# Eight expert groups on one core: slots turned between the up halves, 256-column up products, rank sums shared with VectorE

## What is computed

```
mod = silu(c) @ wmod -> sa, ca, ga, sb, cb, gb       (ga, gb pushed away from 0)
h = layernorm(x) * (1 + ca) + sa ;  x = x + ga * attention(h)     (causal, one head of 256)
h = layernorm(x) * (1 + cb) + sb ;  x = x + gb * ffn(h)

ffn(h):  scores = sigmoid(h @ gate_w.T); best 2 of 4 groups, best 4 of their 16 experts
         weight of a rank = 2 * score / sum of the four scores
         expert e (32 of them, at most 64 tokens each):
             out = (silu(t @ w1[e]) * (t @ w3[e])) @ w2[e]     w1, w3: 256x128, w2: 128x256
         + shared expert: silu(h @ shared_gate) * (h @ shared_up) @ shared_down   (256 wide)
```

## Time and profile before

| what | us |
|---|---|
| median of 3 runs | 176.83 |
| the three runs | 175.35, 176.83, 176.85 |
| the profiled execution | 175.42 |
| its span (first to last instruction) | 173.7 |
| busy in the span: PE, DVE, ACT, POOL | 147.5, 108.9, 62.4, 55.4 |
| first `expert_up` starts | 116.42 |
| first map matmul of the tail (L1391) starts | 153.33 |
| last DVE operation starts | 171.09 |

### The profile page before, as it was taken

One profiled execution on the slowest core, in us unless ns is written; L12 is line 12 of the kernel. 1 busy time (PEld: TensorE's weight loads), 2 busy tenths in 40 slices (PEclk: granted clock), 3 DMA queues, 4 the chain that ended last, 5 costly groups with the idle time before them and its releaser, 6 DMA issues.

```text
span 173.7 us, 2811 instructions
## 1 busy us (share of the span) xinstructions
PE 147.5 (85%) x938; PEld 102.1 (59%) x938; DVE 108.9 (63%) x386; ACT 62.4 (36%) x167; POOL 55.4 (32%) x77
## 2 busy tenths in 40 slices
PE   0198769999999899997598969996999989879993
PEld 0153534887547767685274624886666656568882
DVE  2679964836955688799884598382566664321563
ACT  3257578633055526375243623012333333200000
POOL 7319700499500000000000000777077776440000
PEclk9999999999999999999999999999999999999999
DMA  4999999999999942001000110244113331118995
GB/s 130 340 321 405 423 400 357 348 349 347 349 348 348 348 136 70 0 0 38 30 4 0 44 60 4 68 123 115 36 37 101 94 73 69 50 46 298 411 319 181
DMA packets 21808, 31.34 MB, mean 180 GB/s; under 512 B 2032, under 2 KB 17942, under 8 KB 21794
## 3 DMA queue, kind: packets, MB, share of 16 engines
q1 hardware_dynamic: 20354, 27.71, 46.8%
q0 software_dynamic: 1440, 3.45, 7.2%
HBM read 23.65 MB, written 8.26 MB: 184 GB/s over the span
## 4 chain that ended last, share of the span: by engine, by line
PE 50%; DVE 32%; ACT 7%; issue 5%; DMA 3%; SPq 1%; DVEq 0%; ACTq 0%
PE bank L1054 16%; PE bank L1351 10%; PE bank L1397 6%; PE bank L1391 4%; DMA w_sb<-in_L_wmod_dram 3%; PE bank L1370 3%; DVE bmax L797 3%; DVE st L708 2%; DVE rows L818 2%; PE bank L1184 2%; PE bank L1361 2%; DVE base L811 2%; PE bank L1328 2%; PE bank L1158 2%; PE bank L1162 2%
## 5 line engine op out<-in xcount | busy, mean ns | idle before, releaser
L444 POOL DMA_INDIRECT arena<-token_rows,gather_idx x16 | 16.4, 1025 | 67.2 <-DVE gather_idx L907 62.6
L1351 PE MATMUL bank<-w_sb,arena 128*64 128x128 f32 x256 | 17.3, 278 | 3.4 <-ACT arena L655 1.3
L1351 PEld LDWEIGHTS bank<-w_sb,arena 128*64 128x64 f32 x256 | 13.9, 136 | 7.7 <-issue 4.1
L453 POOL DMA_INDIRECT results<-aT,res_idx x14 | 14.0, 999 | 11.0 <-DVE aT L997 7.9
L1184 PE MATMUL bank<-arena 128*128 128x256 f32 x72 | 17.2, 382 | 0.3 <-issue 0.3
L1184 PEld LDWEIGHTS bank<-arena 128*128 128x128 f32 x72 | 13.1, 190 | 2.5 <-issue 0.9
L1054 PE MATMUL bank<-w_sb,h2T 128*128 128x512 f32 x12 | 7.6, 769 | 8.2 <-DMA w_sb<-in_L_wmod_dram 8.2
L1017 DVE TENSOR_TENSOR h2T<-h2T,bank 128x256 f32<-128x256 f32 x8 | 3.4, 421 | 15.7 <-ACT h2T L672 15.7
L537 ACT ACTIVATE prob<-bank,nmax 128x512 f32<-128x512 f32 (+3 forms) x12 | 6.9, 581 | 12.4 <-DVE nmax L801 12.4
L1397 PE MATMUL bank<-w_sb,ident 128*128 128x256 f32 x48 | 10.6, 382 | 0.0
L556 ACT ACTIVATE h2T<-bank,modc 128x128 f32<-128x128 f32 x16 | 6.4, 455 | 11.5 <-PE bank L1192 11.5
(11 more groups left out here) (154 smaller groups left out, 302.2 us busy)
## 6 DMA issues: line engine op xcount, KB each, us to landing
w_sb<-in_L_ffn_w_dram SPq DMA_DIRECT2D x12, 1024.0 KB, 12.3
results<-prob SPq DMA_DIRECT2D x1, 4096.0 KB, 16.7
w_sb<-results SPq DMA_DIRECT2D x7, 512.0 KB, 6.4
token_rows<-rows SPq DMA_DIRECT2D x8, 144.0 KB
xin<-in_L_attn_x_dram SPq DMA_DIRECT2D x4, 256.0 KB, 4.3
w_sb<-in_L_wmod_dram SPq DMA_DIRECT2D x1, 1024.0 KB, 9.5
out_dram<-base SPq DMA_DIRECT2D x8, 128.0 KB, 3.7
w_sb<-in_L_attn_qkv_dram SPq DMA_DIRECT2D x1, 768.0 KB, 7.1
```

The costliest lines, as they stand in the source:

```text
L444: nc.gpsimd.indirect_dma_start(out=slot_in[:, r, :], out_offset=None, in_=rows_d, in_offset=bass.IndirectOffsetOnAxis(ap=gather_idx[:, r:r ...
L453: nc.gpsimd.indirect_dma_start(out=results_d, out_offset=bass.IndirectOffsetOnAxis(ap=res_idx[:, r:r + 1], axis=0), in_=ob[:, g % 4, (r % ...
L1351: last = t.matmul(bank[4 + g % 2][CAP * side:CAP * side + CAP, o:o + F], slotT[:, k, CAP * e:CAP * e + CAP], w[:, e, k, :], start=(k == 0) ...
```

## The change

- `w1_sb` and `w3_sb` become one buffer `w13_sb` in which w1 and w3 of an expert stand side by side; an up product moves 256 columns (w1 and w3 at once, two pieces of 128 columns that lie 256 floats apart), 16 records for a group in place of 32.
- PE's order in a group is now: `expert_up(g, 0)`, `turn_hid(g - 1)`, `turn_slots(g + 1)`, `expert_up(g, 1)`, `expert_down(g - 1)`. ACT and DVE turn `slot_evac(g + 1)` ahead of silu and product. The copies of scores and `score_sums` stand behind DVE's product.
- `shared_down(3)` goes to the last group, in halves, one on each side of `turn_hid(7)`; for that `ob` gets buffers of its own, and the banks of `SHD_BANK` change.
- `positions(2)` and `map_slots(1, ...)` each stand one `shared_up_part` later.
- POOL gathers groups 0 to 5 ahead of the first give_back (`AHEAD` = 5).
- In the tail PE adds two ranks (three for the last tile), DVE two (one for the last); the maps go over tiles 1 to 7 and then 0.

```diff
--- before.py
+++ after.py
@@ -70,8 +70,7 @@
-        w1_sb = sb("w1_sb", [P, E, KT, F])
-        w3_sb = sb("w3_sb", [P, E, KT, F])
+        w13_sb = sb("w13_sb", [P, E, 2, KT, F])
         w2_sb = sb("w2_sb", [P, E, H])
...
-        flat = lambda t, k: t.rearrange("p e k f -> p (e k f)") if k else t.rearrange("p e n -> p (e n)")
-        place1, place3, place2 = flat(w1_sb[:, last_q], 1), flat(w3_sb[:, last_q], 1), flat(w2_sb[:, last_q], 0)
+        place13 = w13_sb[:, last_q].rearrange("p e w k f -> p (e w k f)")
+        place1, place3 = place13[:, 0:2048], place13[:, 2048:4096]
+        place2 = w2_sb[:, last_q].rearrange("p e n -> p (e n)")
         wmod_a = place3[:, 0:1024].rearrange("p (k n) -> p k n", k=KT)
@@ -136,7 +136,7 @@
         slotT = take(KT * E * CAP).rearrange("p (k s) -> p k s", k=KT)
-        ob = aT[:, :, :].rearrange("p f n -> p (f n)").rearrange("p (b s) -> p b s", b=4)
+        ob = [take(512) for _ in range(3)] + [aT[:, 0, 0:512]]
         silu_c = h2T[:, 0, 0:256].rearrange("p (k n) -> p k n", k=KT)
...
-        yin = [w1_sb[:, 4 * i:4 * i + 4].rearrange("p e k f -> p (e k f)") for i in range(NT)]
+        yin = [w13_sb[:, 2 * i:2 * i + 2].rearrange("p e w k f -> p (e w k f)") for i in range(NT)]
         sh_act = prob[:, :, :].rearrange("p b n -> p (b n)").rearrange("p (b n) -> p b n", n=512)
@@ -302,7 +302,8 @@
         SH_BANK = {key: bank[b] for key, b in zip(SH_ORDER, (0, 1, 2, 3, 6, 4, 5, 0))}
-        SHD_BANK = [bank[b] for b in (1, 2, 4, 5)]
+        SHD_BANK = [bank[b] for b in (1, 2, 3, 0)]
+        PE_RANKS = [2] * (NT - 1) + [3]
         esum = sb("esum", [P, NT, 2])
@@ -354,10 +355,9 @@
                     sp.wait_ge(qT_mm, 2)
-                sp.dma_start(w1_sb[:, e], w1[e].rearrange("e (p k) f -> p e (k f)", k=KT)
-                             .rearrange("p e (k f) -> p e k f", k=KT)).then_inc(experts_loaded[g], 16)
-                sp.dma_start(w3_sb[:, e], w3[e].rearrange("e (p k) f -> p e (k f)", k=KT)
-                             .rearrange("p e (k f) -> p e k f", k=KT)).then_inc(experts_loaded[g], 16)
+                for what, w_d in enumerate((w1, w3)):
+                    sp.dma_start(w13_sb[:, e, what], w_d[e].rearrange("e (p k) f -> p e (k f)", k=KT)
+                                 .rearrange("p e (k f) -> p e k f", k=KT)).then_inc(experts_loaded[g], 16)
                 sp.dma_start(w2_sb[:, e], w2[e].rearrange("e p n -> p e n")).then_inc(experts_loaded[g], 16)
@@ -452,10 +452,10 @@
                         out=results_d, out_offset=bass.IndirectOffsetOnAxis(ap=res_idx[:, r:r + 1], axis=0),
-                        in_=ob[:, g % 4, (r % 2) * H:(r % 2 + 1) * H], in_offset=None,
+                        in_=ob[g % 4][:, (r % 2) * H:(r % 2 + 1) * H], in_offset=None,
                         bounds_check=N * TOPK - 1, oob_is_err=False).then_inc(returned[g % 4], 16)
-            AHEAD = 4
+            AHEAD = 5
             for g in range(EGROUPS):
@@ -666,13 +666,13 @@
                     hid_evac(g - 1)
+                if g + 1 < EGROUPS:
+                    slot_evac(g + 1)
                 act.wait_ge(up_mm, g + 1)
...
                              ACT.Silu).then_inc(silu_done, 1)
-                if g + 1 < EGROUPS:
-                    slot_evac(g + 1)
             hid_evac(EGROUPS - 1)
@@ -975,64 +975,75 @@
             shared_add(1)
-            score_sums()
-            shared_add(2)
...
                 dve.wait_ge(slotT_mm, g + 1)
+                v.tensor_scalar(slotT[:, 1, 256 * g:256 * g + 256], bank[1][:, 0:256],
+                                modc[:, 0, 1:2], modc[:, 1, 1:2], ALU.mult, ALU.add).then_inc(slotT_dve, 1)
+
+            def scores_of_slots(g):
+
                 for side in range(2):
...
                                        slot_flat[half, (2 * g) * (ROW + 2) + H + side::ROW + 2][:, 0:2]))
-                v.tensor_scalar(slotT[:, 1, 256 * g:256 * g + 256], bank[1][:, 0:256],
-                                modc[:, 0, 1:2], modc[:, 1, 1:2], ALU.mult, ALU.add).then_inc(slotT_dve, 1)
-
...
-
-            slot_evac(0)
-            shared_add(3)
-            dve.wait_ge(base_done, NB)
-            dve.wait_ge(scale_done, 1)
-            for g in range(EGROUPS):
+
+            def expert_hid(g):
+
                 dve.wait_ge(silu_done, g + 1)
...
                                 ALU.mult).then_inc(hid_done, 1)
-                if g + 1 < EGROUPS:
-                    slot_evac(g + 1)
-                if g >= 1:
+
+            def expert_evac(g):
+
+                dve.wait_ge(down_mm, g + 1)
+                if g >= 4:
+                    dve.wait_ge(returned[g % 4], 16 * 2 * (g // 4))
+                settle()
+                for r in range(2):
+                    last = v.scalar_tensor_tensor(out=ob[g % 4][:, H * r:H * r + H], in0=bank[6 + g % 2][:, H * r:H * r + H],
+                                                  scalar=slot_score[:, 2 * g + r:2 * g + r + 1], in1=mod[:, 5, :],
+                                                  op0=ALU.mult, op1=ALU.mult)
+                last.then_inc(ob_done, 1)
+
...
+
+            slot_evac(0)
+            shared_add(2)
+            for g in range(EGROUPS - 1):
+                slot_evac(g + 1)
+                expert_hid(g)
+                scores_of_slots(g)
+                if g == 0:
+                    score_sums()
+                else:
                     expert_evac(g - 1)
...
                     back_map(2 * g - 1)
+            scores_of_slots(EGROUPS - 1)
+            expert_evac(EGROUPS - 2)
+            expert_hid(EGROUPS - 1)
             expert_evac(EGROUPS - 1)
-
+            shared_add(3)
+            dve.wait_ge(base_done, NB)
+            dve.wait_ge(scale_done, 1)
...
                     dve.wait_ge(y_rest_loaded, 16)
-                chain(v.scalar_tensor_tensor(out=base[:, i, :], in0=yin[i][:, H * 3:H * 4],
-                                             scalar=scale2[:, i:i + 1], in1=base[:, i, :], op0=ALU.mult, op1=ALU.add))
+                for k in range(PE_RANKS[i], TOPK):
+                    chain(v.scalar_tensor_tensor(out=base[:, i, :], in0=yin[i][:, H * k:H * k + H],
+                                                 scalar=scale2[:, i:i + 1], in1=base[:, i, :], op0=ALU.mult, op1=ALU.add))
                 dve.wait_ge(sum_mm, i + 1)
@@ -1284,16 +1295,17 @@
-            def shared_down(j):
+            def shared_down(j, parts=(0, 1)):
...
                     pe.wait_ge(sh_silu, 2)
-                for i in range(2):
+                for i in parts:
                     tok = slice(P * (2 * j + i), P * (2 * j + i) + P)
...
                                                                      for f in range(FS // P)])
-                last.then_inc(shd_mm, 1)
+                if 1 in parts:
+                    last.then_inc(shd_mm, 1)
@@ -1304,11 +1316,11 @@
             shared_up_part(SH_ORDER[5])
+            shared_up_part(SH_ORDER[6])
             positions(2)
-            shared_up_part(SH_ORDER[6])
-            map_slots(1, BATCHES[2][0], NT, 3)
             pe.wait_ge(sh_silu, 1)
             shared_up_part(SH_ORDER[7])
+            map_slots(1, BATCHES[2][0], NT, 3)
             pe.wait_ge(shd_scaled, 1)
@@ -1321,7 +1333,7 @@
                     pe.wait_ge(ridx_done, 1)
-                    pe.wait_ge(base_done, 2)
+                    pe.wait_ge(base_done, 1)
                     pe.wait_ge(sh_hid, 4)
@@ -1329,34 +1341,30 @@
-            def expert_up(g):
-
-
-                if g % 2 == 0:
-                    pe.wait_ge(experts_loaded[g // 2], 48)
-                pe.wait_ge(slotT_act, g + 1)
-                pe.wait_ge(slotT_dve, g + 1)
-                if g >= 2:
-                    pe.wait_ge(hid_done, g - 1)
-                else:
-                    pe.wait_ge(base_done, 3 + g)
-                for r in range(2):
-                    for what, w in enumerate((w1_sb, w3_sb)):
-                        if g >= 1 and (r, what) == (1, 1):
-                            turn_hid(g - 1)
-                        o = 256 * r + P * what
-                        for k in range(KT):
-                            for side in range(2):
-                                e = 4 * g + 2 * r + side
-                                last = t.matmul(bank[4 + g % 2][CAP * side:CAP * side + CAP, o:o + F],
-                                                slotT[:, k, CAP * e:CAP * e + CAP], w[:, e, k, :],
-                                                start=(k == 0), stop=(k == KT - 1))
-                last.then_inc(up_mm, 1)
+            def expert_up(g, r):
+
+                if r == 0:
+                    if g % 2 == 0:
+                        pe.wait_ge(experts_loaded[g // 2], 48)
+                    pe.wait_ge(slotT_act, g + 1)
+                    pe.wait_ge(slotT_dve, g + 1)
+                    if g >= 2:
+                        pe.wait_ge(hid_done, g - 1)
+                for k in range(KT):
+                    for side in range(2):
```

(41 more changed lines are left out.)

13 lines of the change are left out of this document (6 added, 7 removed).

## The result

The changed kernel takes 170.62 us (median of four, 170.51 to 172.6), the kernel before, run beside it, 176.6 (175.35 to 176.85): ratio 0.9701, 95% interval 0.9617 to 0.9786. The forecast was 170.5. The profiled execution took 170.63 us with a span of 168.9; the forecast for that span was 168.0.

The account below looks back on a forecast made before the run. PE was taken to bound the expert loop and the tail, there nearly tied with loads. Terms took 5.7 us off the span, giving 169.7 us profiled or 171.1 against the median; forecast 170.5, range 168.0 to 174.0.

Parts of the forecast that it names:

- The order ahead of the experts: Work before the expert loop: filling PE's two idle gaps brings the first up block forward, gain 1.1 us.
- One group: Expert loop: PE pays columns, not records; fewer width changes and no slot wait cut the period from 4.44 to 3.5 us.
- A rule that speaks for more: PE's matmuls: 60 cycles overhead per record would bring an estimated 3.2 us; given no part in the forecast.
- Gathers: POOL's calls run without idle; PE stalls 0.8 us at `turn_slots(7)`; maps at 147.7, where they were at 153.33.
- The tail: Final sums after the maps: DVE takes PE's place at 1.42 us a tile, so the moved rank gains nothing.
- The sum: Whole kernel: 5.7 us off the span, 173.7 to 168.0; profiled execution 175.4 to 169.7; forecast 170.5.
- two bases: Starting points for the whole time: the profiled execution gives 169.7 us, the median of runs 171.1.
- A period of 4.0 (1): Expert loop: hidden part or DVE's queue sets the group, 4.0 us; time 172.4 to 173.2; chance 0.17.
- the second base: Whole time reckoned from the median of the runs shown instead of the profiled execution: 171.1 us.
- Loads setting the tail (2): Tail: loads and PE, not DVE, set the pace; time 168.1 to 169.5 us; chance 0.13.
- The strided operand (3): Up products: two-piece moving operand runs below one column a step; slower, 183.5 us if pairs double; chance 0.06.
- POOL's calls (4): Gathers and give_backs stretch to 1.5 us each from 1.32, cancelling the early gain; within 1%; chance 0.05.

Follow-up runs that it names:

- front_old: Changed kernel with `positions(2)` and `map_slots(1, ...)` each one `shared_up_part` earlier, as before the change: 169.38 us, ratio to the kernel before 0.9591.
- before_up256: Kernel before with only `w13_sb` and 256-column up products, order, gathers and tail as before: 176.77 us, ratio to the kernel before 1.0007.
- down128: Changed kernel with `expert_down` products cut into two of 128 columns, 64 more matmul records: 170.88 us, ratio to the kernel before 0.9709.
- order_old: Changed kernel with `turn_slots(g + 1)` behind `expert_up(g, 1)` and `slot_evac` behind `expert_hid(g)` again: 181.48 us, ratio to the kernel before 0.9499.
- ranks3: Changed kernel with PE adding three ranks of every tile in the tail and DVE one, as before: 182.33 us, kernel before beside it 191.6.
- best: Changed kernel with `shared_down(3)` halves around `turn_slots(0)`, PE ranks two and three by turns, six gathers ahead: 178.41 us, ratio to the kernel before 0.9354.
- ahead6: Changed kernel with `AHEAD` = 6 in place of 5: 182.67 us, kernel before beside it 191.6.
- up128_b: Changed kernel with 128-column up products, run a second time, now beside the unmodified changed kernel: 187.74 us, ratio to the kernel before 0.9864.
- the third comparison: Runs on a chip without the long unnamed waits: the unmodified changed kernel 170.79 us, the kernel before 176.62 us, and three edited kernels.
- ahead4: Changed kernel with `AHEAD` = 4 in place of 5: 183.37 us, kernel before beside it 191.6.
- up128: Changed kernel with each 256-column up product cut into two of 128, 32 records a group: 189.37 us, ratio to the kernel before 0.9897.
- the first comparison: First set of follow-up runs, editing products, ranks and gathers ahead, beside the kernel before at 191.6 us, without the unmodified changed kernel.
- after_again: The changed kernel, unmodified, rerun beside the kernel before at 190.71 us: 179.9 us, ratio 0.9414.

## Why the prediction was right

**The order ahead of the experts.** Right in mechanism, small errors in size. The forecast had `positions(2)` late by 0.25 us; PE starts it 0.13 us behind the reduction's end (104.15 + 0.80 to 105.08), where it was 0.05: late by 0.08. `turn_slots(0)` waits for the first gather, as said, and the first up block starts 116.29 - 104.15 = 12.14 us behind the reduction, where it was 13.51: 1.37 us gained, 1.1 forecast. But the step counted this as a gain at the end as well, through group starts set by PE, while giving 0.8 us of it back at `turn_slots(7)`. front_old shows that all of it is given back. I had the parts for that conclusion and didn't draw it. When the last gather is what PE waits for, work that doesn't make the gathers earlier is worth nothing.

**One group.** Forecast 3.5 us, measured 3.55. Its first term, that columns are paid and not records, was put to both sides (before_up256, down128) and held to 0.02 us a block. The two pieces 256 floats apart carry no price either: four pairs take (126.05 - 125.19) / 4 = 0.215 us each in contiguous `w2_sb` and (125.19 - 124.27) / 4 = 0.23, with the start-up behind the transposes, in `w13_sb`. The split of the gain was put as 0.4 wait, 0.2 changes of width and the rest ramps; order_old leaves 0.41 us for the wait with DVE's order and gives 0.51 for the place of `turn_slots`, 0.15 of it in the transposes and up to 0.22 in what is left of the wait for slots.

**A rule that speaks for more.** That each matmul carries about 60 cycles of overhead (the Trainium skill, TensorEngine Tiling (Array Packing), Instruction Overhead) would have meant an estimated 3.2 us off. It got no part, and the runs agree with that: 1.0007 with 128 records fewer, and no change with 64 records more in down128. The next line of that section of the Trainium skill, by which a matmul of one column takes as long as one of 60, makes it the least time of a small matmul and not a sum on top of its columns; so read, it contradicts nothing here.

**Gathers.** This term rests on `AHEAD` = 5, which no run tested on a chip without the long waits. POOL without a gap, as put: 1.32 us a call, last call 148.03 - 1.24 = 146.8 with the dip taken off (147.0 forecast), loads 149.3 (149.5). The new wait ahead of `turn_slots(7)` was forecast as 0.8 us; it came as 0.66: `turn_hid` ahead of it starts at 137.66, `turn_slots(7)` at 138.59, and in an undisturbed group they are 123.74 - 123.47 = 0.27 apart. Maps at 147.4 without the dip, 147.7 forecast. Two small slips stand in the working and changed nothing: 108.67 + 12 x 1.31 + 0.2 is 124.6, the start of the next call and not the end of the twelfth (124.3), and from 136.6 to 137.3 the stall is 0.7 us.

**The tail.** 1.42 us a tile forecast, 1.44 measured, DVE without waits, and nothing gained by the moved rank: ranks3 has 18.12 us against 18.13. "At the same pace" was loose: PE's own pace with three ranks is 1.30 us a tile, and the tie comes about as worked out under ranks3. That a mixture of two and three ranks takes 1.18 us off (best) lay in the same terms and wasn't seen.

**The sum.** The span came out 0.9 us above the forecast 168.0: 1.24 for the clock dip, less 0.3 for the maps. The steps said nothing of a dip, since the earlier trace rows had none. They gave 169.7 us for a profiled execution that took 170.63. That the median still fell only 0.12 us from the forecast is in part luck: 170.5 was put between two bases, and it was not worked out what makes the higher one higher.

**The rivals.** A period of 4.0 (1) did not come, but order_old has just that, 4.06, when ACT's and DVE's part comes after the up block: it was a real edge. Its upper price was mis-added: by the second base, 171.1, 2.7 us more are 173.8 and not 173.2. Loads setting the tail (2) did not come: DVE waits for one load ahead of PE's first sum and none behind. PE does wait for two (0.15 and 0.44 us), which DVE's slower pace hides. The strided operand (3) carries no price. POOL's calls (4) kept 1.32 us.

## What to carry to other kernels

When a loop on one engine is shortened, follow the supply of its last iteration at once: here PE ran into the eighth gather, and the reordering at the front, correct in itself, was worth nothing at the end. On a chip without the long waits told below, merging matmuls was worth only the columns it saves, here none. The shorter group comes from moving a hand-over (turn, empty, use) to where a half block of other work covers it, and it pays only as long as the gathers are far enough ahead. Where work is split between two engines at a tie, moving a whole unit just swaps which one waits: a mixture wins what neither pure split does.

## What the runs showed of the hardware

**A dip of the clock in some executions.** After the same wait of 2.02 us on PE, TensorE fell to 1.2 GHz in the profiled execution of after, from about 87.0 to 90.5, and not in that of before. By the starts of PE's blocks on either side (0.25 us ahead, then 1.23 behind) that cost 1.48 us. It is not the change that brings it: of the fourteen traces seven have it, and down128, best, ranks3, ahead6 and up128_b, which are all the changed kernel with one or more edits, don't. The mask reduction ahead of the experts tells the two kinds apart: it starts at 103.89 to 104.80 in the seven with the dip and at 102.03 to 103.04 in the seven without. What decides it stays open. PE's busy time in the two us ahead of 86 doesn't: it is 0.00 to 0.67 us with the dip and 0.07 to 0.62 without.

Executions of one kernel seem to differ in the same way: in the third comparison six runs of the kernel before had a mean clock of 1.0 and took 174.95 to 176.98 us (median 175.7), seven had 0.99 and took 176.4 to 177.61 (median 176.62). That the latter had this same dip is argued, not shown. A trace of one execution can thus be 1 us off before any change is read, and a row ahead of the change, here the mask reduction, is the one to count from.

**Two chips with long unnamed waits.** The kernel before took 191.6 and 190.71 us on two chips, and 176.6 in the other two comparisons. In the traces from the former, ACT and DVE wait up to 8.3 us (ACT in ahead4) without a named engine while POOL issues gathers and give_backs. The Silu at 120.97 above starts 2.2 us after the end of its up block by PE's timeline (117.70 + 1.03), where 0.1 is usual (119.02 in after, with the block from 117.89). TensorE's clock falls after some of these waits. The changed kernel loses 9 us there and the kernel before 14, so the ratio goes from 0.970 to 0.941. The loss grew with the number of PE's records in the one edit that tried it: 128 more of them, which cost nothing in an undisturbed group, cost 7.8 us in all. From mask reduction to maps that trace has 61.97 us against 53.83, so all of it lies there. The up128 of the first comparison agrees (189.37 us, and 182.33 for ranks3, which has the wide products). PE's busy time and clock in two stretches of 8 us, first after_again, then up128_b:

```profile
120.00:128.00 8.00, 4.45 (x26) 2.25 (x28) 2.84 (x10) 1.59 (x4) 3.98 (x4) 0.71 0.37 97
...
136.00:144.00 8.00, 4.94 (x41) 2.79 (x39) 3.50 (x13) 1.50 (x4) 5.47 (x6) 1.00 0.35 85
```

```profile
120.00:128.00 8.00, 3.72 (x26) 3.20 (x28) 2.42 (x8) 1.55 (x4) 2.59 (x3) 0.68 0.29 74
...
136.00:144.00 8.00, 3.94 (x26) 2.56 (x27) 1.22 (x5) 1.32 (x3) 4.36 (x5) 0.75 0.35 85
```

In these two stretches PE is idle for 16 - 9.39 = 6.6 us in the one and 16 - 7.66 = 8.3 in the other, and the clock is under full in both of the latter's and in one of the former's. What makes the waits stays open: no run here had the same chip with gathers left out or with fewer semaphore events. What can be said is that the wide products, worth nothing on a chip without these waits, were worth several us on one with them, in the changed kernel; the kernel before wasn't run with wide products there.
